# First attention's planes cast by ACT and DVE, second attention's constants set by DVE, weight pieces nine slots apart

## The reference

```python
x = L0_attn_x                                   # (8, 512, 256)
# first attention, for each batch and head
scores_euclid = q @ k.T / sqrt(D)
q_hyp, k_hyp = _expmap0(qn), _expmap0(kn)       # sinh of the norms, time and space parts
dist = arccosh(max(-inner(q_hyp, k_hyp), 1 + 1e-6))
scores = (1 - alpha) * scores_euclid + alpha * (-(dist * dist) / curv_k)
attn = softmax(where(causal, scores, -inf)) * spike_mask
x = _layernorm(x + (attn @ v) @ Wout.T + bout)
# second block
h = _layernorm(x) ; q, k, v = h @ Wq, h @ Wk, h @ Wv
x1 = x + softmax(q @ k.T / sqrt(D)) @ v @ Wo
m = _layernorm(x1)
wts, idx = top_k(softmax(m @ Wg), 2)            # of 8 experts
moe = sum(wts * (gelu(m @ W1[idx] + b1) @ W2[idx] + b2))
x = _layernorm(x + x1 + moe)
```

## Time and profile before

| | |
|---|---|
| median of 3 executions | 2524.64 us (2520.67 to 2529.24) |
| the profiled execution | 2528.54 us, of which the span is 2526.8 us |
| PE busy in the span | 2123.9 us (84%) |
| DVE busy | 1605.6 us (64%) |
| ACT busy | 1493.4 us (59%) |
| POOL busy | 613.4 us (24%) |
| mean granted clock of PE | 0.835 |

### The profile page before, as it was taken

How to read it: one execution, slowest core, us unless ns; L and a number is a source line. 1 busy time by engine, 2 the same in 40 slices (tenths; PEclk the granted TensorE clock), 3 DMA queues, 4 the chain that set the end, 5 groups by cost and what they waited for, 6 DMA issues and landing times. The chain is left out here.

```text
span 2526.8 us, 38830 instructions
## 1 busy us (share of the span) xinstructions
PE 2123.9 (84%) x12343; PEld 1132.9 (45%) x12344; DVE 1605.6 (64%) x3493; ACT 1493.4 (59%) x2762; POOL 613.4 (24%) x638
## 2 busy tenths in 40 slices
PE   4599899989898989994688988888885399999991
PEld 2244444545454444442222322222222288888880
DVE  4576877878787877672566556666652555555556
ACT  1487887888787878882156555565564143333332
POOL 4321314041413232014111122112012133333320
PEclk9677897979897968787689878887777599999995
DMA  1220202121211111100502222452434811111116
GB/s 46 71 64 17 79 18 63 39 59 43 59 43 55 47 51 43 34 9 17 84 18 43 43 51 68 109 143 79 108 108 144 331 67 44 48 44 48 46 38 208
DMA packets 140067, 172.35 MB, mean 68 GB/s; under 512 B 23874, under 2 KB 120339, under 8 KB 137875
## 3 DMA queue, kind: packets, MB, share of 16 engines
q1 hardware_dynamic: 131426, 149.58, 21.3%
q0 software_dynamic: 7488, 20.46, 2.7%
q10 hardware_dynamic: 1008, 0.54, 0.1%
HBM read 105.47 MB, written 65.01 MB: 67 GB/s over the span
## 5 line engine op out<-in xcount | busy, mean ns | idle before, releaser
L1243 DVE TENSOR_REDUCE NM<-sP 128x1 f32<-128x512 f32 x512 | 332.9, 684 | 241.5 <-PE sP L1126 239.6
L1058 ACT ACTIVATE PT<-tP 128x512 f32<-128x512 f32 x512 | 285.7, 604 | 264.9 <-PE tP L1138 263.0
L674 DVE CUSTOM_DVE_ANT_0 YZ<-SeP,YZ 128x512 f32<-128x512 f32 (+3 forms) x512 | 243.5, 487 | 196.4 <-PE SeP L541 179.2
L476 ACT ACTIVATE YZ<-YZ,gsc 128x512 f32<-128x512 f32 (+3 forms) x512 | 325.6, 663 | 69.4 <-DVE YZ L663 69.1
L1489 ACT ACTIVATE H<-hP,B1T 128x256 f32<-128x256 f32 x312 | 127.0, 473 | 271.0 <-PE hP L1568 209.0
L566 PE MATMUL tPa<-ident,YZ 128*128 128x128 f32 x1280 | 258.0, 323 | 1.2 <-ACT PTa L462 0.8
L454 ACT ACTIVATE XL<-mP 128x512 f32<-128x512 f32 (+1 forms) x384 | 204.9, 534 | 63.6 <-PE mP L551 63.3
L462 ACT ACTIVATE PTa<-tPa 128x512 f32<-128x512 f32 (+1 forms) x384 | 207.6, 541 | 41.9 <-PE tPa L572 37.7
L540 PE MATMUL SeP<-STG 48*128 48x512 f16 (+3 forms) x512 | 172.6, 337 | 50.7 <-DVE mn L674 49.5
L663 DVE SCALAR_TENSOR_TENSOR YZ<-YZ,XL 128x1280 f32<-128x1280 f32 x128 | 198.8, 1553 | 21.0 <-ACT YZ L468 19.6
L1126 PE MATMUL sP<-STGb 48*128 48x512 f16 x512 | 171.0, 449 | 46.2 <-DVE NM L1243 36.0
(11 more groups left out here) (301 smaller groups left out, 3994.4 us busy)
## 6 DMA issues: line engine op xcount, KB each, us to landing
STG<-planes_a_scratch SPq DMA_DIRECT2D x512, 32.0 KB, 1.9
X<-in_L_ffn_W SPq DMA_DIRECT2D x32, 512.0 KB, 4.2
weight_planes<-X SPq DMA_DIRECT2D x64, 256.0 KB, 2.5
STGb<-planes_scratch SPq DMA_DIRECT2D x96, 128.0 KB, 6.9
planes_a_scratch<-HI SPq DMA_DIRECT2D x64, 128.0 KB, 1.7
planes_a_scratch<-LO SPq DMA_DIRECT2D x64, 128.0 KB, 1.8
STG<-planes_a_scratch SPq DMA_DIRECT2D x128, 64.0 KB, 2.1
Y<-results_scratch SPq DMA_DIRECT2D x16, 512.0 KB, 8.8
```

The lines of the kernel that those rows point to most:

```text
L476: act.activation(w, w, ACT.Square, bias=gsc[:, b % 2, 1, i, hh:hh + 1], scale=gsc[:, b % 2, 0, i, hh:hh + 1]).then_inc(hyp_ready, 1)
L674: dve.tensor_tensor_reduce(out=w, in0=SeP[tc % 2][:, 0:W[i]], in1=w, scale=1.0, scalar=3e38, op0=ALU.add, op1=ALU.min, accum_out=mn[:, h % ...
L1058: act.activation(PT[:, p % 4, par, kt, :], tP[x % 3][:, :], ACT.Exp).then_inc(exp_done, 1)
L1243: dve.tensor_reduce(NM[:, g % 2, col:col + 1], sP[n % 2][:, :], AX.X, ALU.max, negate=True).then_inc(max_done, 1)
```

## The change

It has three parts. (1) In the first attention ACT writes the high plane `HI` straight from the bank, and DVE makes the low plane `LO` from the bank and `HI` two slots after the transposes; DVE's instruction is the one that frees the bank. `QF` and POOL's two instructions per piece are gone. ACT now waits for the store of the planes two pieces back. (2) In the second attention POOL's fill of `STGb` moves to DVE, behind the first batch's norm factors, with a semaphore `stg_set` for which only SP's first load of `STGb` waits; the waits for all loads move to the first instructions that need them. (3) Weight pieces come every 9 slots instead of every 11, and each piece's store is written 7 slots after its load instead of 10.

```diff
@@ -127,7 +127,6 @@
     spk = sb(ctx, "spk", [P, 3, NT])
-    QF = sb(ctx, "QFa", [P, 2, T])
     HI = sb(ctx, "HI", [P, 2, T], F16)
@@ -282,7 +281,6 @@
     hi_ready = sem("hi_ready")
-    lo_ready = sem("lo_ready")
     pl_stored = [sem(f"pl_stored_a{i}") for i in range(2)]
@@ -364,7 +362,7 @@
                             sp.wait_ge(staged[g % STGS], 320 * (g // STGS + 1))
-                    sp.wait_ge(lo_ready, u + 1)
+                    sp.wait_ge(pb_out, nth[kind, i, b] + 1)
                     row = UNIT[kind] + i
@@ -418,14 +416,6 @@
                                                ALU.mult).then_inc(space_ready, 1)
-                for kind, i, b in pieces(n, 2, "keh"):
-                    u = units[kind, i, b]
-                    pool.wait_ge(pb_out, nth[kind, i, b] + 1)
-                    if u >= 2:
-                        pool.wait_ge(pl_stored[u % 2], 32 * (u // 2))
-                    pool.tensor_copy(HI[:, u % 2, :], QF[:, u % 2, :]).then_inc(hi_ready, 1)
-                    pool.wait_ge(hi_ready, u + 1)
-                    pool.tensor_tensor(LO[:, u % 2, :], QF[:, u % 2, :], HI[:, u % 2, :], ALU.subtract).then_inc(lo_ready, 1)
                 b = at_batch(n, 100)
@@ -491,8 +481,8 @@
                         if u >= 2:
-                            act.wait_ge(lo_ready, u - 1)
-                        act.activation(QF[:, u % 2, :], mis[:, :], ACT.Copy).then_inc(pb_out, 1)
+                            act.wait_ge(pl_stored[u % 2], 32 * (u // 2))
+                        act.activation(HI[:, u % 2, :], mis[:, :], ACT.Copy).then_inc(hi_ready, 1)
                 b = at_batch(n, -52)
@@ -698,6 +688,10 @@
                                       ALU.mult).then_inc(yb_ready, 1)
+                for kind, i, b in pieces(n, 2, "keh"):
+                    u = units[kind, i, b]
+                    dve.wait_ge(hi_ready, u + 1)
+                    dve.tensor_tensor(LO[:, u % 2, :], mis[:, :], HI[:, u % 2, :], ALU.subtract).then_inc(pb_out, 1)
                 for kind, i, b in pieces(n, 1, "qa") + pieces(n, 2, "vw"):
@@ -840,6 +834,7 @@
     b_set = sem("b_set")
+    stg_set = sem("stg_set")
     stored_m = sem("stored_m")
@@ -897,7 +892,7 @@
         d = n - slot(NP + 25, t)
-        return d // 11 if d % 11 == 0 and 0 <= d // 11 < WPIECES else None
+        return d // 9 if d % 9 == 0 and 0 <= d // 9 < WPIECES else None
@@ -930,8 +925,6 @@
             sp.dma_start(WG[:, :, :], a["L0_ffn_Wg"].rearrange("(k p) c -> p k c", p=P)).then_inc(b_loaded, 16)
-            sp.wait_ge(b_set, 3)
-
             for n in range(BEGIN, END):
@@ -942,7 +935,7 @@
                     sp.dma_start(WST.rearrange("p (k c) -> p k c", c=w.shape[2]), w).then_inc(wst_loaded, 16)
-                k = at_piece(n, 10)
+                k = at_piece(n, 7)
                 if k is not None:
@@ -974,6 +967,8 @@
                         if half == 0:
+                            if b == 0:
+                                sp.wait_ge(stg_set, 2)
                             sp.wait_ge(pl_stored, 32 * b + 32)
@@ -996,10 +991,7 @@
             pool.memset(VS[:, :, :, :, :].rearrange("p s i h d -> p (s i h) d")[:, :, D:32], 0.0).then_inc(b_set, 1)
-            for par in range(2):
-                pool.wait_ge(b_set, 1 + par)
-                pool.memset(STG[64 * par + 32:64 * par + 64, :, 1, :, :], SHIFT).then_inc(b_set, 1)
-            pool.wait_ge(b_set, 3)
+            pool.wait_ge(b_set, 1)
             pool.memset(VS[:, :, :, :, :].rearrange("p s i h d -> p (s i h) d")[:, :, D:D + 1], 1.0).then_inc(b_set, 1)
@@ -1040,8 +1032,6 @@
         def _(act):
-            act.wait_ge(b_loaded, 144)
-            act.wait_ge(b_set, 4)
             for n in range(BEGIN, END):
@@ -1078,6 +1068,8 @@
                     if kind == "h":
+                        if u == 0:
+                            act.wait_ge(b_loaded, 144)
                         act.activation(hT[:, b % 2, i, :], src[:, :], ACT.Identity, scale=gcol[:, 0, i:i + 1],
@@ -1106,8 +1098,7 @@
         def _(pe):
-            pe.wait_ge(b_loaded, 144)
-            pe.wait_ge(b_set, 4)
+            pe.wait_ge(b_set, 2)
@@ -1181,6 +1172,8 @@
                         pe.wait_ge(bank_out, nth["h", 1, b] + 1)
+                        if b == 0 and i == 0:
+                            pe.wait_ge(b_loaded, 144)
                         for k in range(CH):
@@ -1227,8 +1220,10 @@
-            dve.wait_ge(b_set, 4)
             for n in range(BEGIN, END):
+                if n == slot(-14, 4):
+                    for par in range(2):
+                        dve.memset(STG[64 * par + 32:64 * par + 64, :, 1, :, :], SHIFT).then_inc(stg_set, 1)
                 k = at_piece(n, 5)
```

## The result

The changed kernel takes 2563.24 us (median of 4 runs, 2555.66 to 2571.66) and the kernel before 2523.2 beside it: ratio 1.0144, 95% interval 1.0107 to 1.0181. It is slower by 40 us, where I forecast 15.8 us less. The profiled execution is the slowest of the four (2571.66 us, span 2569.6, 42.8 more than before).

The account below looks back on a forecast made before the run. No engine is full throughout the two attention loops; the stretch between them and the tail are single chains. Terms +7 - 16.4 - 6.4 = -15.8 us, carried to the runs' median of 2524.64, gave 2509 us (2494 to 2523).

Parts of the forecast that it names:

- Part 1, the loop: First attention's batches: PE waits longer for banks that DVE frees, 0.5 us a batch, +3.5 us in all.
- 0.3 us for each of 56 releases (+17): First attention's loop: upper bound on what PE loses to later bank releases, against a lower bound of -11 us.
- DVE's work: First attention's loop: 56 LO ops add 34 us to DVE; 7.6 to 50 us come back from less POOL contention.
- The run-in: Single chain before the first attention's first head: LO ops delay h0 by 3.3 us, net +3.5 us.
- Part 2: Head of second attention: DVE starts without waiting for POOL's fill, memsets (10.5 to 19 us) stay hidden, -16.4 us.
- Part 3: Second attention and tail: weight pieces at nine slots shorten the tail but load the loop, net -6.4 us.
- +7.7: Second attention's loop: six weight pieces moved in from the tail cost 1.3 us each.
- Parts 2 and 3 together: Constants off the second attention's head (-16.4 us) and weight pieces at nine slots (-6.4 us).
- PE starves: Rival, first attention: each of 56 releases costs 1.6 us, 2595 us in all; slower from 0.48 us a release; chance 0.08.
- longer than 1076: Sign of a wrong forecast: first attention takes over 1076 us from first to last product.
- over 20: Sign of a wrong forecast: PE's waits for LO in the first attention sum to over 20 us.

Follow-up runs that it names:

- after_fill: Changed kernel plus two PE products nobody reads (512 and 256 columns) in the idle after the last h piece, h3: 2527.7 us, ratio 1.0009 to before.
- act_frees: Changed kernel, but ACT also copies the bank to QF, which frees it, and DVE makes LO from that copy: 2561.6 us, ratio 1.0161 to before.
- after_fill_all: Changed kernel plus PE products nobody reads in all of its longer PE idles of the first attention: 2510.8 us, ratio 0.9928 to before.
- planes_only: Kernel before with only the first attention's planes changed (high by ACT, low by DVE): 2572.7 us (2527.4 to 2594.9), ratio 1.0024 to before.

## Why the prediction was wrong

I gave 2509 us (2494 to 2523) and 0.08 to "slower"; it is 2563. Point by point:

- **Part 1, the loop: the step that failed** is "I take 0.5 us a batch for it, the other releases landing where PE or ACT waits anyway: 7 x 0.5 = 3.5 us", with its upper bound of "0.3 us for each of 56 releases (+17)". As a sum of waits it was too low but inside the bounds: with the clock held (after_fill) slots 30 to 60 of batch 4 take 23.7 + 28.2 us, 1.4 more than before. What the step left out is that an idle of PE also costs what the clock does afterwards. PE's idle for one release, that of h3, grew from 0.55 to 1.48 us, and behind it PE ran at 1.2 GHz for 23.9 us, 9 us a batch. Filling that idle takes off 1.35 points, 34 us. Of part 1's 55 us some 20 stay, of which the forecast had 7; about 12 are accounted for above, and the rest is open. I had read the granted clock of the stages (the earlier trace rows has it) and made no term of it.
- **DVE's work** was right. The 56 ops took 38.4 us (forecast 34), and DVE's busy time stayed the same, so the other work took 39 us less once POOL's two instructions per piece were gone (7.6 to 50). L677's mean is 844 ns, "towards 850". The Trainium skill, cited there (SBUF — State Buffer, "Who interferes with whom"), says that such an op does not contend with POOL, and the trace agrees as far as it goes: L694, with one operand in PSUM, has 681 to 692 ns in all 64, though only 7 of them ran beside one of POOL's tensor instructions.
- **The run-in** was right as a chain: v0's product at 65.35 (66.4 forecast), h0 at 74.66 (75.1; the forecast's own terms, 66.4 and twice 4.25, give 74.9). The first scores came 8.2 us later than before in this execution, 3.3 in the mean over the profiled kernels of either kind (111.6 us in six with `LO` on DVE, act_frees apart, 108.3 in seven without).
- **Part 2** was right: 18.0 us between barrier and first scores, 16.4 forecast. The memsets took 6.88 us each, 13.8 of my 10.5 to 19: 0.84 ns an element. The Trainium skill (VectorE: DVE Perf Modes, "Zero memsets can be issued as uint32 (trn2)") has one cycle for each element; at the 0.96 GHz that the same page gives for VectorE this would be 8.5 us each, an estimate. The measured time is shorter, and it decides. They held nothing up that PE waited for; the last thing that PE waited for was the loads of `STGb`.
- **Part 3** was mis-sized in the term "+7.7" for six pieces in the loop: it measures 10.4 us, 1.7 a piece, and the tail gave 12.7 us from the last exponential to the last logits (14.1 forecast), of which 8.8 arrive at the last stage. The sum is about nothing.
- **Parts 2 and 3 together:** forecast -22.8, measured 0.74% of 2536.7, -18.8 us.
- **The rivals.** "PE starves" had the right sign and the wrong mechanism. Its threshold, 0.48 us a release, was about reached: PE waits 29.2 us for 56 releases, 0.52 each, or 0.44 less the 4.4 us that it waited for ACT's copies at these places before. But PE's idle time as a whole fell, and moving one release in eight takes most of the loss away, so the number of releases is not the main thing. The signs that I named were seen: from first to last product 1093.0 us ("longer than 1076"; the 1076 were counted from the stage's 1055.7, and the kernel before has 1033.1 by the same measure as the 1093.0), and 29.2 us for `LO` ("over 20").

## What to carry to other kernels

Price an added wait of PE twice: by its length, and by the granted clock behind it; look in the trace for where the clock falls now and what PE did just ahead, and ask whether the change makes another such place. The longest idle in one piece mattered more here than the sum: 0.93 us more in one place of a batch cost 9 us, while PE's idle time as a whole fell by 10. Its length alone doesn't tell, though: behind 1.12 us at slot 28 the clock held. When PE has idle time that can't be removed, products that nobody reads in that place can be cheaper than the idle; they have to fill the wait and not delay the work behind it. When a kernel's runs spread by 2 or 3% and the time follows the mean clock, compare medians of many runs: the one that is profiled may be the shortest of them.

## What the runs showed of the hardware

- An idle of PE of 1.48 us, behind 0.48 us a few products earlier, was followed by 23.9 us at 1.2 GHz, without a gap in PE's work. At this place the clock fell behind each of 22 idles of 1.37 to 2.74 us, for 13.7 to 23.9 us, and behind none of 54 of 0.13 to 0.75 (the table above). Elsewhere the border is not so clean: 1.12 us at slot 28 of before was not followed by a fall, and 0.89 us at slot 40 of act_frees was in two of its batches 2 to 6 and was not in three.
- The clock also falls with no long idle ahead of it. Near slot 12 it falls in most batches of most kernels here, in the changed one behind 37.4 us in which PE was busy for 36.5 at full clock, among them the projections q0 to q3 in 4-byte numbers. Windows of the changed kernel, ahead of this fall and in it:

```profile
626.70:664.10 37.40, 36.52 (x215) 18.99 (x211) 30.28 (x70) 32.61 (x61) 5.27 (x4) 1.00 0.09 22
664.10:688.00 23.90, 22.20 (x80) 10.32 (x80) 22.73 (x61) 16.32 (x31) 2.36 (x4) 0.50 0.16 43
```

  Its cause stays open: no run here changed those products. In after_fill_all's profile the low stretch there is gone in batches 1 and 2 and lasts 3.4 us in batches 3 to 5, which I can't explain. In batches 2 to 4 of the kernel before, 7 to 27 us a batch stood at the lower clock there.
- The same kernel can take 2527 us at a mean granted clock of 0.840 or 2595 at 0.811 (planes_only) on one chip.
- What also stays open is why the clock holds in some batches and not in others of the kernels with filling; each was profiled once.
